# Other places in a pass for the statistics, convolution and projection products and their VectorE steps

## The chip, the core and the metric

One core of one Trainium2 chip runs the whole program. The metric is the device time of an execution in microseconds (us). Five engines work beside each other, each through its own instructions in the order of the program: TensorE (PE, matrix products), VectorE (DVE), ScalarE (ACT), GpSimd (POOL) and SyncE (SP, which here only issues transfers). They wait for one another through semaphores.

## The reference

Four residual layers stand on an input of 256 images, 256 channels and 7 x 7 positions. Each normalises its input in 32 groups of 8 channels before its own work:

```
def _gn(v, G=32, eps=1e-05):
    ...
    m = jnp.mean(g, axis=(2, 3, 4), keepdims=True)
    s = jnp.var(g, axis=(2, 3, 4), keepdims=True)
    return ((g - m) / jnp.sqrt(s + eps)).reshape(v.shape)
...
x = x + _L0_conv_ref(_gn(x), ...)   # 1x1 convolution with gathered weights
x = x + _L1_conv_ref(_gn(x), ...)   # qkv, depthwise 5x5 and grouped 1x1 of it, linear attention, projection
x = x + _L2_conv_ref(_gn(x), ...)   # a gate for each group and position
x = x + _L3_conv_ref(_gn(x), ...)   # softmax attention over positions
```

The second layer computes `qkv`, from it `agg` (depthwise 5 x 5, then a grouped 1 x 1 product), and for each of 48 heads of the two together `relu(q) (relu(k) v)`, divided by its last column; a projection follows.

## The kernel before

The images go through in 16 chunks of 16. Three phases follow one another: a setup, `layer_one_phase` (layers 0 and 1, and the statistics of layer 2) and `gate_and_attention_phase`. The change is in `layer_one_phase` alone.

That phase is one sequence of steps `g`, written out by each engine for itself. Eight steps make a pass `c = g // 8`; `u = g % 8` is the step in the pass. In passes 0 to 15 (the first half) a pass does the attention on the `qkv` of chunk `c`; in passes 16 to 31 (the second half) that on `agg`. An attention step is spread over five steps of the sequence: PE makes two `qkv` products and turns `q` (L351, L361), then the `vk` product of two steps before (L392), the output product of three steps before (L404) and the turn of the output of four steps before (L413). ACT copies the `qkv` products out of their banks (L667), the `q` (L686), the two `v` (L673) and the turned output `o` (L711); DVE makes `kT` (L492), the masked `vk` pair (L499, L503) and the normalised output (L509 to L514).

Each step has three slots, `a` (PE: after the `qkv` products, DVE: after `kT`), `b` (after the output product; after the `vk` pair) and `c` (after the output's turn; after the normalised output). Two tables, `PE_AT` and `V_AT`, say what else is done in which slot. "5c" below is slot c of step 5 in a pass. An entry is (what, number, how many passes ahead of its own chunk's). For a chunk and layer `k` (0 or 1) the chain is:

- DVE `sum` (L533), PE `stat` (a product with a mask, L437), DVE `centre` (reads the mean, L537, then subtracts it, L547), ACT `a_square` (L722), DVE `square_sum` (L552), PE `stat` again, DVE `var` (L555), ACT `a_root` (L728), DVE `scale` (four short instructions from L561 on, then L571).
- After layer 0's chain: PE `l0` (four convolution products, L445), each read by DVE (L577), whose result is the input of layer 1's chain. After layer 1's chain the next pass's `qkv` products can begin.
- For the chunk of the pass before: PE `proj` (four projection products, L452), read by DVE (L588).

The `stat`, `l0` and `proj` products, and those for the gate, share two PSUM banks in turn. Before a product writes its bank, PE waits until the product two turns before has been read:

```
            i = turn[what, n, k]
            bank = p_g[i % 2]
            wait(pe, pg_read, i - 1)
```

`turn` is counted from `PE_AT`. ACT's squares and roots have their places in `a_step`, by `u`. One buffer `sq` takes all squares, and `stat[:, 0]` and `stat[:, 1]` take both the sum and the square sum of a layer in turn.

From step 4 of pass 8 to step 2 of pass 15, and again in the second half's first 44 steps, there are fills: depthwise products of PE (L426, two or three a step), which go to one bank and are copied out by ACT (L694) before the next may start. Their input is gathered by POOL (L834) and their weights come by DMA.

Of the kernel before, what the change touches and what calls it, by code (L numbers as in the profile page):

```python
# [191 lines left out]
def layer_one_phase(nc, bass, mybir, ins, W, dram, chunks):  # L192
# [8 lines left out]
    with ctx:  # L201
        def sb(name, shape):
            return ctx.enter_context(nc.sbuf_tensor(name, shape, f32))
# [26 lines left out]
        stat = sb("stat", [128, 2, KT * NB])  # L230
        mean = sb("mean", [128, KT, NB])
        var = sb("var", [128, KT * NB])
# [73 lines left out]
        def fill_in(g, slot):  # L306

            mine = fills.get(g, [])
            return mine[slot] if slot < len(mine) else None

        PE_AT = {(0, "a"): [("stat", 1, 1)], (1, "c"): [("l0", 0, 1)], (2, "a"): [("gate_stat", 0, -2), ("l0", 1, 1)], (2, "b"): [("l0", 2, 1)],
                 (3, "a"): [("l0", 3, 1)], (5, "c"): [("gate_stat", 1, -2)],
                 (4, "b"): [("stat", 2, 1)], (4, "c"): [("proj", 0, -1)],
                 (6, "a"): [("stat", 3, 1), ("stat", 0, 2)], (6, "b"): [("proj", 1, -1)], (6, "c"): [("proj", 2, -1)],
                 (7, "b"): [("proj", 3, -1)]}
        V_AT = {(0, "a"): [("proj", 3, -2)], (0, "b"): [("var", 0, 1)], (0, "c"): [("gate_sum", 0, -2)],
# [3 lines left out]
                (5, "b"): [("proj", 0, -1), ("sum", 0, 2)], (5, "c"): [("square_sum", 1, 1)],  # L320
                (6, "b"): [("var", 1, 1), ("centre", 0, 2)], (6, "c"): [("proj", 1, -1)],
                (7, "a"): [("scale", 1, 1)], (7, "b"): [("proj", 2, -1)], (7, "c"): [("gate_scale", 0, -2), ("square_sum", 0, 2)]}

        def due(table, g, slot):

            for what, k, ahead in table.get((g % UN, slot), ()):
                n = g // UN + ahead
                if what == "proj":
                    here = 0 <= n < NP2
                elif what.startswith("gate"):  # L330
                    here = chunks <= n < NP2
                else:
                    here = 0 <= n < chunks
                if here:
                    yield what, n, k

        turn = {}
        for g in range(FIRST, LAST + 1):
            for slot in "abc":
                for key in due(PE_AT, g, slot):  # L340
                    turn[key] = len(turn)
# [88 lines left out]
        def pe_group(pe, what, n, k):  # L430
# [4 lines that stand above are left out]
            if what == "stat":  # L435
                pe.wait_ge(summed[k // 2], 2 * n + k % 2 + 1)
                mm = pe.matmul(bank[:, 0:KT * NB], W["mask8"][:, :], stat[:, k // 2, :], start=True, stop=True)  # L437
            elif what == "gate_stat":
                pe.wait_ge(gate_summed, 2 * (n - chunks) + k + 1)
                mm = pe.matmul(bank[:, 0:KT * NB], W["mask8"][:, :], stat[:, k, :], start=True, stop=True)  # L440
            elif what == "l0":
                m, h = k // 2, k % 2
                pe.wait_ge(scaled[0], n + 1)
                for t in range(KT):
                    mm = pe.matmul(bank[:, 0:HALF], W["w_sub"][:, t, 128 * m:128 * m + 128],  # L445
                                   y[:, t, HALF * h:HALF * h + HALF], start=(t == 0), stop=(t == KT - 1))
            else:
                m, h = k // 2, k % 2
                pe.wait_ge(o_ev, UN * (n + 1))
                q0 = 0 if n < chunks else 2  # L450
                for e in range(2):
                    mm = pe.matmul(bank[:, 0:HALF], W["w_proj"][:, q0 + e, 128 * m:128 * m + 128],  # L452
                                   o[:, n % 2, e, HALF * h:HALF * h + HALF], start=(e == 0), stop=(e == 1))
            mm.then_inc(pg_mm, 1)

        def pe_slot(pe, g, slot):
            for what, n, k in due(PE_AT, g, slot):
                pe_group(pe, what, n, k)
# [181 lines left out]
        def v_slot(v, g, slot):  # L640
            for what, n, k in due(V_AT, g, slot):
                if what.startswith("gate"):
                    v_gate(v, what, n)
                else:
                    v_group(v, what, n, k)
# [69 lines left out]
        def a_square(a, n, k):  # L715
            a.wait_ge(centred[k], n + 1)

            if k == 1:
                a.wait_ge(summed[0], 2 * n + 2)
            elif n > 0:  # L720
                a.wait_ge(summed[1], 2 * n)
            a.activation(sq[:, :, :], y if k == 0 else z[n % 2], ACT.Square).then_inc(squared[k], 1)  # L722
# [25 lines left out]
        def a_step(a, g):  # L748
            c, u = g // UN, g % UN

            def fill(slot):
                F = fill_in(g, slot)
                if F is not None:
                    a_fill(a, F)

            for F in fills.get(g - 1, ()):
                if F % DB_FILLS == DB_FILLS - 1:
                    a_store_agg(a, F // DB_FILLS)

            G = g - 1  # L760
            if 0 <= g < GA:
                a_raw(a, g, 0)
            if 0 <= G < GA:
                a_q(a, G)
            if 0 <= g < GA:
                a_raw(a, g, 1)
            if u == 5 and 0 <= c + 1 < chunks:
                a_square(a, c + 1, 1)
            if 0 <= G < GA:
                a.wait_ge(raw_ev, 2 * G + 2)  # L770
                a_v(a, G, raw[:, G % UN // 4, G % 4, 256:384, :].rearrange("r n q -> r q n"))
            elif GA <= G < GT:
                a_kv_of_agg(a, G)
                a_q(a, G)
            fill(0)
            fill(1)
            if 0 <= g - 4 < GT:
                a_out(a, g - 4)
            fill(2)
            if u == 2 and 0 <= c < chunks:  # L780
                a_residual(a, c)
            if u == 6 and 0 <= c + 2 < chunks:
                a_square(a, c + 2, 0)
            if u == 3 and chunks <= c - 2 < NP2:
                a_gate_square(a, c - 2 - chunks)
            if u == 6 and chunks <= c - 2 < NP2:
                a_gate_root(a, c - 2)
            if u in (0, 6) and 0 <= c + 1 < chunks:
                a_root(a, c + 1, u // 6)


# [927 lines left out]
```

## Time and profile before

| | |
|---|---|
| median of 3 runs | 2079.17 us (2075.14 to 2084.48) |
| the profiled execution | 2083.96 us, of it 2082.1 us span from the first to the last instruction |
| busy share of the span | PE 86%, DVE 66%, ACT 43%, POOL 13% |
| setup, and wait for the first chunk | to 69 us |
| first half (passes 0 to 15) | 69 to 922 us |
| second half and the end of the phase | 922 to about 1568 us |
| gate and attention phase | from about 1568 us |

The numbers of the trace are us from the span's start. "Idle before" is the time an engine did nothing before an instruction, with the one whose end released it. The granted clock is PE's, as a share of full speed (2.4 GHz; 0.50 is 1.2 GHz). A pass of the first half is measured from the first `qkv` product on its chunk to the first on the next; the product reads `half_a` and `z_odd` in turn.

### The profile page before, as it was taken

Reading aid. Unit: us, or ns where it says so; the run is one execution under the profiler, and the core shown is the slowest. Engines: PE = TensorE matmul, PEld = TensorE weight load, DVE = VectorE, ACT = ScalarE, POOL = GpSimd, SP = SyncE. Lnnn points to the kernel's source line nnn. Section 1 sums busy time; section 2 is a strip of 40 time slices with the busy share of each in tenths; the row PEclk is TensorE's granted clock in tenths of the full one; section 3 lists DMA queues with packets and bytes.
Section 4 is the critical chain, followed back from the end, with each engine's and each line's share of the span. In section 5 each row is a group of like instructions: output and inputs, shape, how many; then the busy total and the mean of one; then the engine's idle time right before and its main releaser. Section 6 shows DMA issues by size and latency. Waiting matters only on the chain. (4 is left out here: it accounts for less than half of the span.)

```text
span 2082.1 us, 42128 instructions
## 1 busy us (share of the span) xinstructions
PE 1786.3 (86%) x16164; PEld 1195.1 (57%) x16164; DVE 1372.3 (66%) x2786; ACT 901.7 (43%) x2341; POOL 277.0 (13%) x189
## 2 busy tenths in 40 slices
PE   2699999999999999997877888999983499999998
PEld 1355555555555555565555666666661366666666
DVE  4677777666555556442333447777875899999994
ACT  0344454454554544453433445455541144444343
POOL 1000000001111101002111110000001233333331
PEclk9899999999999999998988899999995699999999
DMA  3112222237666667479988986545513001111101
GB/s 100 39 63 78 101 94 78 78 125 185 207 170 199 201 160 215 145 185 218 237 231 219 246 229 166 134 121 149 156 48 128 16 32 63 62 63 63 47 32 47
DMA packets 199916, 267.17 MB, mean 128 GB/s; under 512 B 108516, under 2 KB 159588, under 8 KB 199720
## 3 DMA queue, kind: packets, MB, share of 16 engines
q1 hardware_dynamic: 189320, 225.68, 38.4%
q10 hardware_dynamic: 10240, 38.54, 6.0%
q8 instruction: 132, 2.16, 0.4%
q14 instruction: 64, 0.52, 0.1%
q0 software_dynamic: 160, 0.26, 0.0%
HBM read 148.84 MB, written 115.61 MB: 127 GB/s over the span
## 5 line engine op out<-in xcount | busy, mean ns | idle before, releaser
L499 DVE TENSOR_TENSOR vk<-p_vk,mask_vo 128x512 f32<-128x512 f32 x256 | 176.4, 689 | 478.3 <-PE p_vk L392 478.3
L426 PE MATMUL p_dw<-tw,q 98*64 98x98 f32 x3072 | 198.3, 266 | 86.8 <-ACT agg_out L694 34.9
L834 POOL COPY q<-qd 98x768 f32<-98x768 f32 x128 | 110.5, 900 | 1085.5 <-DMA qd<-qkv_scratch 787.2
L667 ACT ACTIVATE half_b<-p_qkv 98x384 f32<-98x384 f32 x256 | 134.2, 524 | 244.2 <-PE p_qkv L351 229.6
L426 PEld LDWEIGHTS p_dw<-tw,q 98*64 98x64 f32 x3072 | 148.1, 143 | 151.5 <-issue 67.8
L694 ACT ACTIVATE agg_out<-p_dw 128x294 f32<-128x294 f32 x256 | 106.9, 417 | 258.6 <-PE p_dw L426 246.0
L452 PE MATMUL p_g<-o,w_proj 128*128 128x392 f32 x512 | 207.5, 531 | 3.4 <-DVE var L555 2.8
L351 PE MATMUL p_qkv<-w_qkv,half_a 128*98 128x384 f32 x512 | 193.8, 502 | 6.7 <-DVE half_a L571 6.7
L351 PE MATMUL p_qkv<-w_qkv,z_odd 128*98 128x384 f32 x512 | 190.2, 494 | 1.8 <-DVE z_odd L571 1.8
L404 PE MATMUL p_out<-vk,qr 128*49 128x136 f32 x2048 | 170.5, 287 | 8.5 <-DVE oN L514 5.4
L711 ACT ACTIVATE o<-p_turn 128x196 f32<-128x196 f32 x256 | 85.5, 334 | 167.5 <-PE p_turn L413 166.1
L1360 PE MATMUL p_b<-wv,z 128*98 128x256 f32 x512 | 121.2, 385 | 8.0 <-DVE x L1235 8.0
L413 PE MATMUL p_turn<-ident,oN 128*128 128x128 f32 x512 | 111.1, 300 | 19.1 <-ACT qr L686 17.4
L673 ACT ACTIVATE vT<-half_b,image_of 98x256 f32<-98x256 f32 x256 | 124.4, 538 | 0.0
L404 PEld LDWEIGHTS p_out<-vk,qr 128*49 128x49 f32 x2048 | 110.3, 125 | 24.3 <-issue 10.0
L452 PEld LDWEIGHTS p_g<-o,w_proj 128*128 128x128 f32 x512 | 91.8, 199 | 56.2 <-issue 16.8
L392 PEld LDWEIGHTS p_vk<-vT,kT 98*32 98x32 f32 x4096 | 71.6, 109 | 89.4 <-issue 85.0
L392 PE MATMUL p_vk<-vT,kT 98*32 98x66 f32 x4096 | 114.2, 228 | 3.4 <-DVE vk L503 3.2
L514 DVE TENSOR_TENSOR oN<-p_out,rden 128x256 f32<-128x256 f32 x256 | 108.6, 424 | 8.8
L351 PEld LDWEIGHTS p_qkv<-w_qkv,half_a 128*98 128x98 f32 x512 | 81.0, 174 | 57.4 <-issue 47.0
L351 PEld LDWEIGHTS p_qkv<-w_qkv,z_odd 128*98 128x98 f32 x512 | 79.8, 171 | 50.7 <-issue 44.9
L673 ACT ACTIVATE vT<-p_qkv,image_of 98x256 f32<-98x256 f32 x256 | 106.9, 474 | 0.0
(192 smaller groups left out, 3202.4 us busy)
## 6 DMA issues: line engine op xcount, KB each, us to landing
qkv_scratch<-half_b SPq DMA_DIRECT2D x32, 1176.0 KB
qd<-qkv_scratch SPq DMA_DIRECT2D x64, 588.0 KB
agg_scratch<-agg_out ACTq DMA_DIRECT2D x128, 294.0 KB, 5.8
tw<-in_w_toep SPq DMA_DIRECT2D x128, 220.5 KB
half_a<-agg_scratch SPq DMA_DIRECT2D x48, 392.0 KB, 6.9
half_b<-agg_scratch SPq DMA_DIRECT2D x48, 392.0 KB, 6.8
half_a<-in_x SPq DMA_DIRECT2D x16, 784.0 KB, 4.9
x_scratch<-xb SPq DMA_DIRECT2D x16, 784.0 KB, 4.8
```

Source lines behind the costliest of these rows:

```text
L351: mm = pe.matmul(p_qkv[r][0:PR, 0:QKV], z[c % 2][:, t, PR * w:PR * w + PR], W["w_qkv"][:, t, QKV * e:QKV * e + QKV], start=(t == 0), stop= ...
L392: mm = pe.matmul(p_vk[32 * c:32 * c + 32, 2 * VC * pr:2 * VC * pr + 2 * VC], kT[:, G % 2, pr, 32 * c:32 * c + 32], vT[:, G % 2, pr, :, c, ...
L404: mm = pe.matmul(out_of[64 * i:64 * i + S, pr, 0:VO], qr[:, G % 4, at:at + S], vk[:, G % 2, pr, i, :], start=True, stop=True)
L413: mm = pe.transpose(turned_of[:, pr, 0:128], oN[:, G % 2, pr, :], W["ident"][:, :])
L426: mm = pe.matmul(p_dw[NP * cp:NP * cp + NP, PR * s:PR * s + PR], q2[:, U % Q2, DB_CH * cp + 3 * (f % DB_FILLS) + s, :, :].rearrange("r w q ...
L452: mm = pe.matmul(bank[:, 0:HALF], W["w_proj"][:, q0 + e, 128 * m:128 * m + 128], o[:, n % 2, e, HALF * h:HALF * h + HALF], start=(e == 0), ...
L499: v.tensor_tensor(dst[:, :, 0:128].rearrange("p k (c n) -> p k c n", c=HC), src[:, :, 0:2 * D].unsqueeze(2).to_broadcast([128, 4, HC, 2 * D]),
L514: v.tensor_tensor(oN[:, G % 2, :, :].rearrange("p r (h d) -> p r h d", h=8), out_of[:, :, 0:128].rearrange("p r (h d) -> p r h d", h=8), r ...
L667: a.activation(raw[:, e, g % 4, :, r], p_qkv[r][0:PR, 0:QKV], ACT.Copy).then_inc(raw_ev, 1)
L673: a.activation(vT[:, G % 2, :, i, :, 0:2 * D], src.rearrange("r q (c n) -> r q c n", c=HC), ACT.Copy, scale=W["image_of"][:, i:i + 1]).the ...
L834: g.tensor_copy(q2[:, U % Q2, DB_CH * cp:DB_CH * cp + DB_CH, :, :].rearrange("r n w q -> r w n q"), qd[:, :, at:at + DB_CH, :]).then_inc(q ...
L1360: mm = pe.matmul(p_b[0:PR, n % 2, C * q:C * q + C], two_images(z3[it % Z3S][:, t, :], 2 * n + q), wv[:, t, :], start=(t == 0), stop=(t == ...
```

## The change

Only places change. In the first half, layer 0's chain for the next chunk starts half a step to one step later: `sum` from 5b to 5c, its `stat` from 6a to 6c, `centre` from 6b to 7b, the square from the end of step 6 to the end of step 0 of the next pass, `square_sum` from 7c to 0c, its `stat` from 0a to 1a, `var` from 0b to 1b, `scale` from 1a to 1c. The four `l0` products go from 1c, 2a, 2b, 3a to 2b, 2c, 3a, 3b. In layer 1's chain `square_sum` goes from 5c to 5b, ahead of the next chunk's `sum`. In both halves the projection products 2 and 3 go from 6c and 7b to 7a and 7c on PE; DVE reads them where it did. Of the tables two lines are shown, with the lines of `a_step`:

```diff
-                (5, "b"): [("proj", 0, -1), ("sum", 0, 2)], (5, "c"): [("square_sum", 1, 1)],
...
+                (5, "b"): [("proj", 0, -1), ("square_sum", 1, 1)], (5, "c"): [("sum", 0, 2)], (6, "a"): [("gate_var", 0, -2)],
...
-            if u == 6 and 0 <= c + 2 < chunks:
-                a_square(a, c + 2, 0)
+            if u == 0 and 0 <= c + 1 < chunks:
+                a_square(a, c + 1, 0)
...
-            if u in (0, 6) and 0 <= c + 1 < chunks:
+            if u in (1, 6) and 0 <= c + 1 < chunks:
                 a_root(a, c + 1, u // 6)
```

The line numbers of the changed kernel are two lower from there on. PE, step 6 of pass 1 from its slot a and most of step 7, before (`p_g` is a bank of the shared pair; L437 `stat`, L452 `proj`):

```order
L437 MATMUL p_g<-stat,mask 128x32 x2
L392 MATMUL p_vk<-vT,kT 32x66 x8
L404 MATMUL p_out<-vk,qr 49x136 x4
L452 MATMUL p_g<-o,w_proj 128x392 x2
L413 MATMUL p_turn<-ident,oN 128x128 x2
L452 MATMUL p_g<-o,w_proj 128x392 x2
L351 MATMUL p_qkv<-w_qkv,z_odd 98x384 x2
L361 MATMUL p_turn<-ident,half_b 128x98 x2
L351 MATMUL p_qkv<-w_qkv,z_odd 98x384 x2
L392 MATMUL p_vk<-vT,kT 32x66 x8
L404 MATMUL p_out<-vk,qr 49x136 x4
L452 MATMUL p_g<-o,w_proj 128x392 x2
```

The same stretch of the changed kernel (L435 `stat`, L450 `proj`):

```order
L435 MATMUL p_g<-stat,mask 128x32
L390 MATMUL p_vk<-vT,kT 32x66 x8
L402 MATMUL p_out<-vk,qr 49x136 x4
L450 MATMUL p_g<-o,w_proj 128x392 x2
L411 MATMUL p_turn<-ident,oN 128x128 x2
L435 MATMUL p_g<-stat,mask 128x32
L349 MATMUL p_qkv<-w_qkv,z_odd 98x384 x2
L359 MATMUL p_turn<-ident,half_b 128x98 x2
L349 MATMUL p_qkv<-w_qkv,z_odd 98x384 x2
L450 MATMUL p_g<-o,w_proj 128x392 x2
L390 MATMUL p_vk<-vT,kT 32x66 x8
L402 MATMUL p_out<-vk,qr 49x136 x4
```

The next chunk's `stat` stands at the step's end instead of beside the fourth one, projection product 2 after the `qkv` products of step 7 instead of before them, and product 3 behind the turn that follows the last row.

DVE, step 5 from the `vk` pair and the first part of step 6, in the same pass, before (L533 `sum`, L552 `square_sum`, L537 and L547 `centre`):

```order
L499 TENSOR_TENSOR vk<-p_vk,mask_vo 128x4x128
L503 TENSOR_TENSOR vk<-p_vk,mask_vo 128x4x8
L588 SCALAR_TENSOR_TENSOR xb<-p_g,bn_scale,xb 128x392
L533 TENSOR_REDUCE stat<-half_a 128x32
L509 TENSOR_SCALAR den<-p_out 128x16
L511 RECIPROCAL rden<-den 128x16
L514 TENSOR_TENSOR oN<-p_out,rden 128x256
L552 TENSOR_REDUCE stat<-sq 128x32
L492 TENSOR_SCALAR kT<-half_b 98x256
L499 TENSOR_TENSOR vk<-p_vk,mask_vo 128x4x128
L503 TENSOR_TENSOR vk<-p_vk,mask_vo 128x4x8
L555 TENSOR_SCALAR var<-p_g 128x32
```

The same of the changed kernel (L531 `sum`, L550 `square_sum`):

```order
L497 TENSOR_TENSOR vk<-p_vk,mask_vo 128x4x128
L501 TENSOR_TENSOR vk<-p_vk,mask_vo 128x4x8
L586 SCALAR_TENSOR_TENSOR xb<-p_g,bn_scale,xb 128x392
L550 TENSOR_REDUCE stat<-sq 128x32
L507 TENSOR_SCALAR den<-p_out 128x16
L509 RECIPROCAL rden<-den 128x16
L512 TENSOR_TENSOR oN<-p_out,rden 128x256
L531 TENSOR_REDUCE stat<-half_a 128x32
L490 TENSOR_SCALAR kT<-half_b 98x256
L497 TENSOR_TENSOR vk<-p_vk,mask_vo 128x4x128
L501 TENSOR_TENSOR vk<-p_vk,mask_vo 128x4x8
L553 TENSOR_SCALAR var<-p_g 128x32
```

The two reductions have changed places around the normalised output.

ACT, from the end of step 6 of pass 1 to the end of step 0 of pass 2, before (L711 `o`, L722 the square, L728 the root):

```order
L711 ACTIVATE o<-p_turn 128x196
L722 ACTIVATE sq<-half_a 128x1568
L728 ACTIVATE std<-var 128x32
L667 ACTIVATE half_b<-p_qkv 98x384
L686 ACTIVATE qr<-p_turn 128x196
L667 ACTIVATE half_b<-p_qkv 98x384
L673 ACTIVATE vT<-half_b,image_of 98x2x4x32 x2
L711 ACTIVATE o<-p_turn 128x196
L667 ACTIVATE half_b<-p_qkv 98x384
L686 ACTIVATE qr<-p_turn 128x196
L667 ACTIVATE half_b<-p_qkv 98x384
L673 ACTIVATE vT<-half_b,image_of 98x2x4x32 x2
```

The changed kernel, from the root in step 6 on (L709 `o`, L720 the square, L726 the root):

```order
L726 ACTIVATE std<-var 128x32
L665 ACTIVATE half_b<-p_qkv 98x384
L684 ACTIVATE qr<-p_turn 128x196
L665 ACTIVATE half_b<-p_qkv 98x384
L671 ACTIVATE vT<-half_b,image_of 98x2x4x32 x2
L709 ACTIVATE o<-p_turn 128x196
L665 ACTIVATE half_b<-p_qkv 98x384
L684 ACTIVATE qr<-p_turn 128x196
L665 ACTIVATE half_b<-p_qkv 98x384
L671 ACTIVATE vT<-half_b,image_of 98x2x4x32 x2
L709 ACTIVATE o<-p_turn 128x196
L720 ACTIVATE sq<-half_a 128x1568
```

The square stands behind the copy of `o` in step 0 of pass 2, where the first layer's root stood before; that root is now a step later.

## Rows read from the trace of the kernel before

**Rows 1.** Windows: length, busy (count) by engine, granted clock (PEclk), DMA share, GB/s.

```profile
256.82:303.95 47.13, 44.98 (x330) 25.82 (x329) 34.31 (x77) 23.87 (x54) 0.00 (x0) 1.00 0.25 87
111.66:448.57 336.91, 321.61 (x2296) 184.01 (x2297) 241.17 (x536) 166.50 (x377) 0.00 (x0) 0.98 0.23 82
448.57:755.45 306.88, 290.29 (x2651) 178.56 (x2649) 177.78 (x382) 150.69 (x354) 42.86 (x48) 0.96 0.68 189
755.45:875.87 120.42, 114.54 (x1113) 71.16 (x1111) 68.65 (x151) 60.81 (x146) 14.53 (x16) 1.00 0.58 169
1262.00:1420.00 158.00, 143.81 (x1678) 107.77 (x1682) 121.37 (x304) 81.04 (x229) 0.00 (x0) 1.00 0.58 150
```

**Rows 2.** Time line of PE, step 6 of pass 4: start, length; idle before.

```profile
290.54 0.46 PE L361 MATMUL p_turn<-ident,half_b 98*128 98x98 f32 x2 [0.51 <-ACT o L711]
...
293.53 0.60 PE L437 MATMUL p_g<-stat,mask 128*128 128x32 f32 x4 [1.24 <-DVE stat L552]
...
295.51 1.58 PE L452 MATMUL p_g<-o,w_proj 128*128 128x392 f32 x4 [0.41 <-DVE var L555]
```

**Rows 3.** Time line of DVE, step 5 of the same pass.

```profile
289.08 1.78 DVE L533 TENSOR_REDUCE stat<-half_a 128x32 f32<-128x1568 f32 x1
...
291.61 1.78 DVE L552 TENSOR_REDUCE stat<-sq 128x32 f32<-128x1568 f32 x1
```

**Rows 4.** Time lines of PE and ACT, step 1 of pass 4; a square.

```profile
261.08 1.45 PE L351 MATMUL p_qkv<-w_qkv,half_a 128*98 128x384 f32 x4
...
263.96 0.44 PE L392 MATMUL p_vk<-vT,kT 98*32 98x66 f32 x16
...
265.20 1.52 PE L445 MATMUL p_g<-half_a,w_sub 128*128 128x392 f32 x4
...
265.40 0.34 ACT L711 ACTIVATE o<-p_turn 128x196 f32<-128x196 f32 x1
...
250.45 1.50 ACT L722 ACTIVATE sq<-half_a 128x1568 f32<-128x1568 f32 x1
```

**Rows 5.** Time lines of DVE and PE before the first attention step.

```profile
42.57 0.35 DVE L561 RECIPROCAL root<-std 128x32 f32<-128x32 f32 x1 [0.30 <-ACT std L728]
...
59.55 1.77 DVE L552 TENSOR_REDUCE stat<-sq 128x32 f32<-128x1568 f32 x1
62.11 0.19 DVE L555 TENSOR_SCALAR var<-p_g 128x32 f32<-128x32 f32 x1 [0.79 <-PE p_g L437]
...
66.25 0.35 DVE L561 RECIPROCAL root<-std 128x32 f32<-128x32 f32 x1 [1.70 <-ACT std L728]
...
69.17 4.75 PE L351 MATMUL p_qkv<-w_qkv,half_a 128*98 128x384 f32 x8 [6.66 <-DVE half_a L571]
```

**Rows 6.** Time line of PE, four waits in pass 0.

```profile
77.71 1.55 PE L445 MATMUL p_g<-half_a,w_sub 128*128 128x392 f32 x4 [0.81 <-DVE half_a L571]
...
103.20 0.60 PE L437 MATMUL p_g<-stat,mask 128*128 128x32 f32 x4 [0.70 <-DVE stat L552]
...
109.47 0.41 PE L413 MATMUL p_turn<-ident,oN 128*128 128x128 f32 x2 [0.58 <-ACT qr L686]
...
111.66 1.53 PE L351 MATMUL p_qkv<-w_qkv,z_odd 128*98 128x384 f32 x4 [1.78 <-DVE z_odd L571]
```

**Rows 7.** Time lines of ACT and PE in pass 13, with fills.

```profile
762.58 0.22 ACT L728 ACTIVATE std<-var 128x32 f32<-128x32 f32 x1
...
765.11 0.44 PE L392 MATMUL p_vk<-vT,kT 98*32 98x66 f32 x16
...
767.14 0.73 PE L426 MATMUL p_dw<-tw,q 98*64 98x98 f32 x12 [0.47 <-POOL q L834]
...
798.98 0.73 PE L426 MATMUL p_dw<-tw,q 98*64 98x98 f32 x12 [1.62 <-ACT agg_out L694]
```

**Rows 8.** Time line of PE in the second half, end of a pass.

```profile
1308.89 1.48 PE L452 MATMUL p_g<-o,w_proj 128*128 128x392 f32 x4
...
1314.12 1.04 PE L377 MATMUL p_qkv<-pwbd,half_b 128*98 128x128 f32 x8
```

More of the change, by code:

```diff
@@ L309, in fill_in @@
             return mine[slot] if slot < len(mine) else None
[L311 to L316, printed above, removed]
[3 rows of a table removed]
-                (5, "b"): [("proj", 0, -1), ("sum", 0, 2)], (5, "c"): [("square_sum", 1, 1)],
-                (6, "b"): [("var", 1, 1), ("centre", 0, 2)], (6, "c"): [("proj", 1, -1)],
-                (7, "a"): [("scale", 1, 1)], (7, "b"): [("proj", 2, -1)], (7, "c"): [("gate_scale", 0, -2), ("square_sum", 0, 2)]}
+        PE_AT = {(1, "a"): [("stat", 1, 1)], (2, "a"): [("gate_stat", 0, -2)], (2, "b"): [("l0", 0, 1)], (2, "c"): [("l0", 1, 1)],
[3 rows of a table added]
+        V_AT = {(0, "a"): [("proj", 3, -2)], (0, "c"): [("gate_sum", 0, -2), ("square_sum", 0, 1)], (1, "b"): [("var", 0, 1)],
+                (1, "c"): [("scale", 0, 1)], (2, "c"): [("gate_centre", 0, -2), ("l0", 0, 1)], (3, "a"): [("l0", 1, 1)],
+                (3, "b"): [("l0", 2, 1)], (3, "c"): [("l0", 3, 1), ("sum", 1, 1)], (4, "c"): [("gate_square_sum", 0, -2), ("centre", 1, 1)],
+                (5, "b"): [("proj", 0, -1), ("square_sum", 1, 1)], (5, "c"): [("sum", 0, 2)], (6, "a"): [("gate_var", 0, -2)],
+                (6, "b"): [("var", 1, 1)], (6, "c"): [("proj", 1, -1)], (7, "a"): [("scale", 1, 1)],
+                (7, "b"): [("centre", 0, 2), ("proj", 2, -1)], (7, "c"): [("gate_scale", 0, -2)]}
         def due(table, g, slot):
```

6 rows, old and new, of tables (PE_AT, V_AT) are left out of this document.

## The prediction

> **What bounds the kernel now.** I read the busy times and the granted clock by stretches first, then the waits of TensorE (PE), then the time lines of PE, VectorE (DVE) and ScalarE (ACT) in one pass. All the moved steps lie in layer one, and nearly all that counts in its first half (69 to 922 us), where a pass of eight steps handles one chunk of 16 images. There PE is the bound. In a pass without fills at full clock it is busy 44.98 of 47.13 us, while DVE is busy 34.31 and ACT 23.87 [rows 1]. So a microsecond counts only if PE stood idle in it, or if a wait makes it stand idle.
>
> The idle 2.15 us of such a pass all lies in step 6, in three waits [rows 2], which come back within 0.01 us in each of passes 1 to 7:
> - 0.51 us before the q transpose, for ACT. ACT has just squared the second layer's chunk in step 5, and its copy of `o` is late.
> - 1.24 us before the fourth statistics product. DVE takes the next chunk's sum (from 289.08) ahead of the square sum that PE waits for (from 291.61) [rows 3].
> - 0.41 us before projection product 1, for DVE's read of that product's bank.
>
> There is a second price. Seven passes took 336.91 us, and seven times 47.13 is 329.91. The 7.0 us between them are almost all time at half clock: the granted clock over the stretch is 0.98, not 1.00 [rows 1]. By the same view pass by pass, a stretch at half of full speed (1.2 GHz) follows the three waits in passes 1, 2, 5 and 7, and none in 3, 4 and 6: 7.0 / 4, about 1.7 us lost each time.
>
> From step 4 of pass 8 on, PE also makes the fills (depthwise products), and passes take about 60 us. There PE waits mostly for ACT's eviction of the fill before; one such wait, of about 1.6 us, comes in step 5 of nearly every pass [rows 7].
>
> **The change part by part.** No instruction is added or dropped; steps change places. The second table of order rows shows the heart of it: square sum ahead of sum.
>
> Step 6, passes without fills. The square sum takes the sum's place and can start there (289.08, not 291.61) or as soon as ACT's square ends, over 2 us earlier than now [rows 3]; the 1.24 us go. Projection product 1 now has the fourth product's bank behind it by one more product, so its 0.41 us go too. The 0.51 us stay: the second square keeps its place in step 5.
>
> Step 7. Projection product 3 now needs the bank that the next chunk's mean is read from, and DVE gets to that read only after the `vk` pair. It is the wait of 0.41 us again, with one more pair of transposes on PE ahead of it: 0.2 us, an estimate.
>
> Steps 0 and 1. The first layer's square moves from the end of ACT's step 6 to the end of its step 0, its square sum from DVE's 7c to 0c, and its product from PE's 0a to 1a. This chain used to be spread over a step and a half of slack; now it follows itself closely. A step with nothing extra takes PE 4.12 us (261.08 to 265.20), and ACT starts its copy of `o` 4.32 us into it [rows 4]. So the square starts at 4.32 + 0.34 = 4.66 after step 0 begins, ends 1.50 later, and from the start of a square sum to the product that needs it 1.92 us pass (291.61 to 293.53) [rows 2 to 4]: the product can start at 8.08. PE is there at 4.12 + 2.88 = 7.00 (2.88 is 261.08 to 263.96). A new wait of 1.1 us. DVE is behind the same square, so the scaling after it, moved to 1c, ends level with PE's arrival at the first convolution product in 2b: 0.1 us, an estimate. Queued behind DVE's wait at 0c are the `kT` of step 1 and the scaling, for which PE waits no longer than said. Behind the square on ACT stands the eviction of step 1's first qkv product, and PE needs that bank only in step 2. No DMA moves; SP's loads and stores wait for the same steps as before.
>
> Per pass without fills: 0.5 + 0.2 + 1.1 + 0.1 = 1.9 in place of 2.15. Seven passes: -1.8 us. The wait is moved rather than removed.
>
> Passes with fills (8 to 14). In step 6 there is nothing to win, for PE shows no wait at its statistics product there. The new wait is there all the same: ACT is free at 762.58 (where it now takes the first root), so the product could start at 762.58 + 1.50 + 1.92 = 766.00, and PE is there at 765.11 [rows 7]: 0.9 us. The product's own 0.2 us come on top, since in step 0 a fill waits for ACT anyway and taking the product out wins nothing. ACT catches up during the wait, so most of the 0.47 us at the next fill goes [rows 7]: minus 0.3. Moving the convolution and projection products changes which fills have a product between them; I make that level. 0.8 us, seven times: +5.6 us. Bounds: nothing (if fills hide it) and 1.2.
>
> The start. Before the first attention step PE waits for a chain on DVE and ACT alone. Now the next chunk's centring and its square stand between the variance (62.11) and its root, and the reciprocal starts at 66.25 [rows 5]. After the change the square sum starts at 59.55 as before, the sum follows (1.70 each, as between the starts in rows 3 and what comes behind), the variance is read at 62.95, and the reciprocal follows 0.19 + 0.30 later, as in the first round [rows 5]: 63.44. -2.8 us. Pass 0 then loses its waits of 0.81, 0.70, 0.58 and 1.78 [rows 6] and gets 1.1 (the new one), 0.35 (first convolution product) and about 1.0 in step 6, where no projection product yet separates the two statistics products and DVE has still the sum, `kT`, `vk` and the variance to do: -1.4 us.
>
> The second half (922 to 1568 us). Only projection products 2 and 3 move on PE. Now product 2 starts at 1308.89, as the last of step 6, and the next pass at 1314.12 [rows 8]. Taking product 2 behind the pointwise products of step 7 and product 3 to that step's end leaves the same work between these two times, and DVE's `vk`, which follows PE's, starts when it did. 0; with fills 0.2 us a pass either way.
>
> The clock. The half-clock stretches in passes 1 to 7 came after three waits close together, 2.15 us within 6. Afterwards the longest cluster is 1.1 us. In neither half did I find one behind a wait of 1.2 us or less that stands apart: from 1262 us on PE is idle 14.2 of 158 us, in waits of about 1 us and less, and the clock is 1.00 [rows 1]. So I take the four stretches as gone: -7.0 us. In passes 8 to 12 the mean clock is 0.96 over 306.88 us, which costs some 0.04 of it, 12 us, in stretches behind waits of 1.6 to 2.0 us; after 755 us the same waits, as the 1.62 us at 798.98, cost no clock (1.00) [rows 1, 7]. I leave those as they are.
>
> **Sum.** -1.8 + 5.6 - 2.8 - 1.4 - 7.0 = -7.4 us. The profiled execution took 2083.96 us (span 2082.1): 2076.6, say 2077. The median of the runs shown is 2079.17, 4.8 below this execution, which may come of fewer half-clock stretches, so less is left to win against it. I call the change level with the median; 0.5% is 10.4 us, about what a measurement of this kernel tells from no change.
>
> **Rivals.**
> 1. The clock stays as it was in passes 1 to 7. The 0.51 us stay and the new wait is nearly as long as the old. For it: identical waits gave a stretch in four passes and not in three. 2083.96 - 0.4 = 2083.6.
> 2. The new wait is hidden, and with it the cluster. If ACT reaches the square sooner than I place it, and the looser order keeps the fill passes at full clock as well: 2076.6 - 5.6 - 12 = 2059; half of both, 2068. Against it: the 1.6 us wait in step 5 has a cause that isn't touched.
> 3. Slower: the short waits throttle every pass. A wait of 1.1 us at the product of step 1, in the middle of a pass that has the 0.51 or the 1.6 us as well, could bring a stretch of half clock to each. At 1.7 us a stretch, seven instead of four in passes 1 to 7 and six more in the fill passes: 2083.6 + 5.1 + 10.2 = 2099. It decides from four added stretches on (2090). Against it: waits in pass 0 of up to 1.78 us were not followed by one [rows 6]. The Trainium skill, page "TensorE: Matmul & The Clock Gate", section "A second HAM failure mode: psum-queue depth-cycling", says that short, frequent idle spells of PE between groups of matmuls can make the clock swing between its two levels, which would give this rival's time; the trace agrees only for waits of 1.5 us and more or for several close together.
> 4. The reorder doesn't reach PE. If the fourth product still comes late because ACT's square ends late, 1.24 us of each pass come back: 2076.6 + 8.7 = 2085. DVE now finds the square done when it comes to it, without a wait [rows 3], so little speaks for it.
>
> **How the numbers follow.** My forecast has 0.45 (its own range 2070 to 2084), rival 1 0.18, rival 2 0.21, rival 3 0.13, rival 4 0.03. Three quarters of rival 2 and a tenth of the forecast lie under 2068.8 (0.20 together); rival 3 lies over 2089.6 (0.13); the rest is within 0.5%. The range of 8 in 10 takes in most of rivals 2 and 3: 2062 to 2091.
>
> **What would show it.** Right: no wait for the square sum in step 6; a wait of about 1 us at the first-layer statistics product of step 1 in nearly every pass up to 14; the first qkv product some 2.8 us earlier; passes 1 to 7 near 46.9 us each, at clock 1.00; fill passes 0.8 us longer at equal clock; the second half the same length. Wrong: fill passes no longer or even shorter, half-clock stretches behind step 1, or a new wait of PE on DVE at the convolution products of step 2.

## The result and the profile after

The changed kernel took 2064.86 us (median of 7 runs, 2060.7 to 2070.3) against 2079.17 us for the kernel before on the same chip (7 runs, 2071.57 to 2084.48): a ratio of 0.9943 [0.992, 0.9965], 0.57% faster (in brackets the 95% interval; the plain quotient of the two medians is 0.9931). The forecast was 2077 us, level with the median; the time lies in its range (2062 to 2091), and just over the bound of 0.5% on the fast side. The profiled execution took 2067.97 us, with a span of 2066.2 in place of 2082.1.

Stretch by stretch, each of the first half measured between the same two `qkv` products in both traces:

| stretch | before | after | difference | forecast |
|---|---|---|---|---|
| start, to the first `qkv` product | 69.17 | 67.65 | -1.5 | -2.8 |
| pass 0 | 42.49 | 40.62 | -1.9 | -1.4 |
| passes 1 to 7 | 336.91 | 326.62 | -10.3 | -8.8 (-1.8 and -7.0) |
| passes 8 to 14 | 427.30 | 429.45 | +2.2 | +5.6 |
| pass 15 | 46.01 | 46.37 | +0.4 | none made |
| second half and last phase | 1160.2 | 1155.5 | -4.7 | 0 |
| sum | | | -15.9 | -7.4 |

The last row runs from the first pointwise product to the end. The windows of the changed kernel that answer to [rows 1] (same columns): pass 0, passes 1 to 7, pass 4 alone, passes 8 to 12, passes 13 and 14.

```profile
67.65:108.27 40.62, 38.47 (x246) 21.00 (x246) 27.03 (x54) 21.40 (x47) 0.00 (x0) 0.94 0.15 50
108.27:434.89 326.62, 316.03 (x2297) 180.67 (x2298) 243.25 (x534) 167.07 (x379) 0.00 (x0) 1.00 0.25 87
248.42:295.04 46.62, 45.12 (x329) 25.79 (x328) 34.60 (x77) 23.82 (x54) 0.00 (x0) 1.00 0.25 87
434.89:740.70 305.81, 286.02 (x2650) 175.81 (x2648) 180.91 (x383) 150.73 (x354) 45.38 (x48) 0.98 0.67 191
740.70:864.34 123.64, 116.41 (x1111) 72.03 (x1110) 70.83 (x153) 61.61 (x145) 14.75 (x16) 0.99 0.53 158
```

Read the granted clock, the third number from the right, first. It is 1.00 over the whole of passes 1 to 7, where it was 0.98. A pass there is 46.62 us instead of 47.13, and PE is idle 1.50 of it instead of 2.15.

The time line of PE in pass 4 and at the start of pass 5 (start, length; idle before), which answers to [rows 2]: the turn of `q` in step 6, the two statistics products of that step (the one for the square sum, then the one for the next chunk's sum), projection product 3 at the end of step 7, and the first layer's product for its square sum, now in step 1.

```profile
283.35 0.45 PE L359 MATMUL p_turn<-ident,half_b 98*128 98x98 f32 x2 [0.50 <-ACT o L709]
...
284.93 0.30 PE L435 MATMUL p_g<-stat,mask 128*128 128x32 f32 x2
...
287.78 0.31 PE L435 MATMUL p_g<-stat,mask 128*128 128x32 f32 x2
...
293.62 1.58 PE L450 MATMUL p_g<-o,w_proj 128*128 128x392 f32 x4
...
303.06 0.38 PE L435 MATMUL p_g<-stat,mask 128*128 128x32 f32 x2 [0.95 <-DVE stat L550]
```

The 0.50 stays, the 1.24 and the 0.41 of [rows 2] are gone, and a wait of 0.95 has come, 20 us further on. What releases it is told by ACT and DVE in the same step 0 of pass 5 (time lines of the two engines):

```profile
299.36 0.33 ACT L709 ACTIVATE o<-p_turn 128x196 f32<-128x196 f32 x1
299.59 1.50 ACT L720 ACTIVATE sq<-half_a 128x1568 f32<-128x1568 f32 x1
...
301.13 1.79 DVE L550 TENSOR_REDUCE stat<-sq 128x32 f32<-128x1568 f32 x1 [1.09 <-ACT sq L720]
```

DVE waits 1.09 us for the square, and PE waits for DVE: the chain runs from ACT to DVE to PE without slack, as the prediction placed it. Step 0 began at 295.04, so `o` is at 4.32, the square at 4.55 (4.66 was forecast) and the product at 8.02 (8.08 was forecast).

The time line of PE in pass 9, with fills:

```profile
494.36 0.73 PE L424 MATMUL p_dw<-tw,q 98*64 98x98 f32 x12 [0.80 <-ACT agg_out L692]
...
499.19 0.38 PE L435 MATMUL p_g<-stat,mask 128*128 128x32 f32 x2 [0.95 <-DVE stat L550]
...
532.61 0.84 PE L424 MATMUL p_dw<-tw,q 98*64 98x98 f32 x12 [1.64 <-ACT agg_out L692]
```

And windows of 2 us behind its last wait (columns as in [rows 1]):

```profile
533.00:535.00 2.00, 2.00 (x23) 1.40 (x18) 1.93 (x5) 0.75 (x2) 0.00 (x0) 0.52 0.73 277
535.00:537.00 2.00, 2.00 (x7) 0.98 (x4) 1.33 (x2) 0.42 (x1) 1.67 (x2) 0.50 0.43 112
```

The new wait came in each fill pass (0.95 us, in two of them 0.87; 6.5 us over the seven), and the clock stayed full behind it. The clock fell to 0.50 (1.2 GHz) behind the wait of 1.64 us for ACT's eviction, which the change does not touch. This happened in passes 9, 12 and 13. Taking one minus the clock times the length, pass by pass, about 8.4 us went to half clock in passes 8 to 14, against 11.8 before: -3.4 by the clock and +5.5 by the rest, where +5.6 was forecast. The parts of that rest agree less well than its sum: PE's waits for ACT's eviction fell from 19.3 to 15.2 us, and its waits for POOL rose from 0.9 to 2.9, of which one in pass 12 is 2.01.

The start, time line of DVE: the reads of the four groups of convolution products, then the sum, the variance and the reciprocal that [rows 5] showed before.

```profile
48.69 0.63 DVE L575 SCALAR_TENSOR_TENSOR half_a<-p_g,b_sub,half_a 128x392 f32<-128x392 f32 x1 [3.13 <-PE p_g L443]
51.30 0.63 DVE L575 SCALAR_TENSOR_TENSOR half_a<-p_g,b_sub,half_a 128x392 f32<-128x392 f32 x1 [1.99 <-PE p_g L443]
52.95 0.62 DVE L575 SCALAR_TENSOR_TENSOR half_a<-p_g,b_sub,half_a 128x392 f32<-128x392 f32 x1 [1.03 <-PE p_g L443]
54.27 0.63 DVE L575 SCALAR_TENSOR_TENSOR half_a<-p_g,b_sub,half_a 128x392 f32<-128x392 f32 x1 [0.69 <-PE p_g L443]
...
62.58 1.78 DVE L531 TENSOR_REDUCE stat<-half_a 128x32 f32<-128x1568 f32 x1
64.27 0.18 DVE L553 TENSOR_SCALAR var<-p_g 128x32 f32<-128x32 f32 x1
64.75 0.35 DVE L559 RECIPROCAL root<-std 128x32 f32<-128x32 f32 x1 [0.29 <-ACT std L726]
```

The sixteen convolution products of PE that these reads follow, in the changed kernel and in the one before, and the last of the four reads before:

```profile
45.70 8.53 PE L443 MATMUL p_g<-half_a,w_sub 128*128 128x392 f32 x16 [3.52 <-DVE half_a L569]
...
45.58 7.30 PE L445 MATMUL p_g<-half_a,w_sub 128*128 128x392 f32 x16 [3.53 <-DVE half_a L571]
...
52.91 0.63 DVE L577 SCALAR_TENSOR_TENSOR half_a<-p_g,b_sub,half_a 128x392 f32<-128x392 f32 x1 [0.69 <-PE p_g L445]
```

From the last of the four reads to the first `qkv` product (67.65) it is now 13.38 us; before, it was 16.26. That is -2.88, the forecast's -2.8. But the four reads themselves span 5.58 us here and spanned 4.34 before, since the sixteen products took 8.53 us in place of 7.30, and so 1.24 came back.

The last row of the table is left open. Windows of before, from the first pointwise product to the end in two parts:

```profile
921.88:1575.00 653.12, 552.57 (x6517) 410.41 (x6515) 367.30 (x916) 285.78 (x803) 53.09 (x64) 0.93 0.68 179
1575.00:2082.00 507.00, 410.46 (x2900) 293.63 (x2900) 439.17 (x644) 184.66 (x549) 157.15 (x48) 0.92 0.15 55
```

The same of the changed kernel:

```profile
910.71:1560.00 649.29, 547.89 (x6516) 407.25 (x6514) 366.70 (x916) 285.99 (x803) 53.74 (x64) 0.94 0.69 179
1560.00:2066.00 506.00, 409.02 (x2900) 292.78 (x2900) 439.97 (x645) 184.68 (x549) 157.16 (x48) 0.93 0.16 56
```

The same products cost PE 6.1 us less (956.9 against 963.0) at a clock 0.01 higher, and the other engines as much as before. Together with the seven profiles below there are nine, one of each kernel. In the four with projection products 2 and 3 at their old places this stretch takes 1160.2 to 1163.3 us, in the five with the new places 1154.9 to 1159.7. By one minus the clock times the length, 86 to 90 us of it went to half clock in the four, and 78 to 85 in the five. So the -4.7 may come of the change, by way of the clock, and not of a difference between executions alone. With one profile of each kernel, and only about 0.5 us between the two groups, that is not shown.

### The profile page after: what moved, and what is told of

Its sections match the earlier page's. It is cut to its first block and busy times, and to the rows that moved or that the text cites. A ratio compares the mean times of both kernels' runs of the same rounds, so it can differ in the third digit from the quotient of the medians.

```text
span 2066.2 us, 42128 instructions
## 1 busy us (share of the span) xinstructions
PE 1773.7 (86%) x16164; PEld 1186.7 (57%) x16164; DVE 1378.0 (67%) x2786; ACT 902.2 (44%) x2341; POOL 280.4 (14%) x189
## 5 line engine op out<-in xcount | busy, mean ns | idle before, releaser
L450 PE MATMUL p_g<-o,w_proj 128*128 128x392 f32 x512 | 199.4, 514 | 0.8 <-ACT o L709 0.5
L709 ACT ACTIVATE o<-p_turn 128x196 f32<-128x196 f32 x256 | 85.5, 334 | 155.2 <-PE p_turn L411 154.4
L402 PEld LDWEIGHTS p_out<-vk,qr 128*49 128x49 f32 x2048 | 109.6, 124 | 24.3 <-issue 10.3
L450 PEld LDWEIGHTS p_g<-o,w_proj 128*128 128x128 f32 x512 | 91.8, 195 | 51.5 <-issue 11.5
```

Source lines behind the costliest of these rows:

```text
L402: mm = pe.matmul(out_of[64 * i:64 * i + S, pr, 0:VO], qr[:, G % 4, at:at + S], vk[:, G % 2, pr, i, :], start=True, stop=True)
```

## The experiments

The theory, called A in the expectations, is the prediction's mechanism as the trace after bears it out: each wait of PE counts at its length times the number of passes, an edit taken back brings its own waits back and no others, and half clock follows waits that are long or lie close together. The rival, B, lets the gain come from elsewhere; each expectation says what it would give there. The median of the kernel before beside them was 2076.99 us for the first two, the fourth and the fifth below, and 2079.4 us for the other three.

**The sum ahead of the square sum again.** In the changed kernel, the two reductions of step 5 change back:

```diff
-                (5, "b"): [("proj", 0, -1), ("square_sum", 1, 1)], (5, "c"): [("sum", 0, 2)], ...
+                (5, "b"): [("proj", 0, -1), ("sum", 0, 2)], (5, "c"): [("square_sum", 1, 1)], ...
```

> The changed kernel with one part undone: in DVE's step 5 the next chunk's sum stands ahead of the square sum again (5b and 5c as before the change); all other places stay as changed. Theory A (the swap is what PE's step 6 needed): the wait of 1.24 us at the fourth statistics product comes back in passes 1 to 7, which go from 46.6 to about 47.9 us at full clock; fill passes unchanged; the start 0.8 us shorter, since the sum no longer stands between square sum and variance: about 8 us more than the changed kernel (2073), and more (up to 12 us) if half-clock stretches come back behind the waits of 0.5 and 1.24 us. Rival B (moving the other products apart did it): no wait of 1 us in step 6, time within 2 us of the changed kernel.

Measured: 2074.93 us, ratio 0.9994 [0.9973, 1.0014]. Its window of passes 1 to 7, and its waits of PE there (us in total, times, longest):

```profile
106.60:443.24 336.64, 317.51 (x2299) 180.05 (x2297) 243.42 (x534) 166.86 (x380) 0.00 (x0) 1.00 0.24 85
```

```profile
PE p_g L435 <- DVE stat L550: 15.4, 14, 1.2
PE p_turn L359 <- ACT o L709: 3.5, 7, 0.5
```

The 1.24 us are back beside the 0.95, and the seven passes cost 10.0 us more than in the changed kernel, 8.7 of them in this wait. So the gain needs the exchange of the two reductions. And a point for the clock: PE is idle 2.7 us a pass here, more than the 2.15 before the change, and no pass has a stretch at half clock.

**That exchange alone, in the kernel before.**

```diff
-                (5, "b"): [("proj", 0, -1), ("sum", 0, 2)], (5, "c"): [("square_sum", 1, 1)],
+                (5, "b"): [("proj", 0, -1), ("square_sum", 1, 1)], (5, "c"): [("sum", 0, 2)],
```

> The kernel before with the swap alone: square sum in DVE's 5b, the next chunk's sum in 5c; all else as before the change, so that the next chunk's first statistics product still stands beside the fourth one at the head of PE's step 6. Theory A (the swap alone moves the wait to the neighbouring product, which needs the sum): PE waits 1.2 to 1.5 us at the second of the two products, passes 1 to 7 stay at 47.1 to 47.5 us plus half-clock stretches, no gain: 2077 to 2083. Rival B (the swap is the whole gain): passes 1 to 7 at 45.9 us, about 2068 or less.

Measured: 2081.11 us, ratio 1.0021 [1.0003, 1.0038]. Its waits of PE in passes 1 to 7:

```profile
PE p_g L437 <- DVE stat L533: 9.8, 7, 1.4
PE p_turn L361 <- ACT o L711: 3.5, 7, 0.5
PE p_g L452 <- DVE var L555: 2.8, 7, 0.4
...
```

The wait has only changed its name: the next chunk's statistics product, which still stands in 6a, now waits 1.4 us for the sum (L533). Three of seven passes had a stretch of half clock (335.84 us in all), and the first `qkv` product came at 71.60, 2.4 later; half of that stands in its sixteen convolution products, which took 8.50 us. So the exchange by itself gains nothing as long as that product stays in 6a. No run has the exchange with that product in 6c and nothing else changed.

**Projection products 2 and 3 back.** In the changed kernel, on PE alone:

```diff
-                 (6, "c"): [("stat", 0, 2)], (7, "a"): [("proj", 2, -1)], (7, "c"): [("proj", 3, -1)]}
+                 (6, "c"): [("stat", 0, 2), ("proj", 2, -1)], (7, "b"): [("proj", 3, -1)]}
```

> The changed kernel with projection products 2 and 3 back at their old places on PE (6c, behind the next chunk's first statistics product, and 7b); all else as changed. Theory A (these moves matter in the first half only, where product 2 would wait for DVE's read of product 1, and product 3 for the read of the mean): new waits of about 0.8 us in step 6 and 0.5 us in step 7, passes 1 to 7 at about 47.9 us in place of 46.6, fill passes up to 0.8 us longer; the stretch from 922 us on (there 1155 to 1160 us in all runs so far) unchanged: 8 to 14 us more than the changed kernel, ratio to the kernel before 0.998 to 1.002. Rival B (their move brought the 4 us that the changed kernel's second half and last phase are shorter in the first profile): the second half 4 us longer, passes 1 to 7 unchanged, ratio 0.996.

Measured: 2077.43 us, ratio 1.0 [0.9973, 1.0027]. Its waits of PE in passes 1 to 7:

```profile
PE p_g L435 <- DVE stat L550: 6.7, 7, 1.0
PE p_g L450 <- DVE xb L586: 5.7, 7, 0.8
PE p_turn L359 <- ACT o L709: 3.5, 7, 0.5
PE p_g L450 <- DVE mean L535: 2.8, 7, 0.4
...
```

Two waits for the shared pair of banks appear, 0.8 and 0.4 us: the product has arrived before DVE has read the one two turns before. The second half, where the same two products went back, took 1160.3 us to the end. That is 4.8 us more than in the changed kernel, about what B expected there, while passes 1 to 7 did not stay unchanged, as B had it; one profile does not settle the second half (see above). So the places of the projection products, which look like a side matter of the change, cost as much as the exchange wins: 1.24 us a pass, 8.7 in passes 1 to 7, and 1.8 in the fill passes (431.21).

**The new wait taken away: the first layer's square a step earlier.** In the changed kernel ACT squares at the end of step 7 of the pass before, instead of at the end of step 0:

```diff
-            if u == 0 and 0 <= c + 1 < chunks:
-                a_square(a, c + 1, 0)
+            if u == 7 and 0 <= c + 2 < chunks:
+                a_square(a, c + 2, 0)
```

> The changed kernel with the first layer's square one place earlier on ACT: at the end of step 7, right behind the centring it needs, in place of the end of step 0. Theory A (the wait of 0.95 us at the statistics product of step 1 is the chain copy of o, square, square sum): the square sum no longer waits, the product of step 1 finds it done, passes 1 to 7 take about 45.7 us, passes 8 to 14 0.7 to 0.9 us less each: 14 us less than the changed kernel, about 2051. Rival B (the square's 1.5 us on ACT only make something else late, as the second layer's square does with 0.5 us and 1.6 us): a new wait of 0.5 to 1.5 us for ACT in step 0, time 2058 to 2065.

Measured: 2051.95 us, ratio 0.9884 [0.9861, 0.9908]. Windows of passes 1 to 7 and of passes 8 to 14:

```profile
107.50:426.46 318.96, 314.39 (x2296) 180.72 (x2297) 242.40 (x534) 168.32 (x379) 0.00 (x0) 1.00 0.25 89
426.46:854.97 428.51, 405.42 (x3759) 250.84 (x3757) 250.42 (x536) 214.06 (x499) 60.18 (x64) 0.97 0.63 182
```

The 0.95 us are gone from every pass (45.42 us each but the first), and nothing takes their place but 0.65 us in pass 1. In the fill passes the wait is gone too, but the profiled execution lost more there to half clock (six of the seven passes have a stretch) and was, at 2062.5, the slowest of this kernel's six. The ratio moved by 0.0059 against the changed kernel's, 12 us, and 0.95 us in 14 passes are 13.3.

**The other wait: the second layer's square first in step 5.** In the changed kernel ACT squares before it copies the `qkv` products of step 5:

```diff
+            if u == 5 and 0 <= c + 1 < chunks:
+                a_square(a, c + 1, 1)
             if 0 <= g < GA:
                 a_raw(a, g, 0)
...
                 a_raw(a, g, 1)
-            if u == 5 and 0 <= c + 1 < chunks:
-                a_square(a, c + 1, 1)
```

> The changed kernel with the second layer's square moved to the start of ACT's step 5, ahead of the evictions of the qkv products, instead of between them and the two v copies. Theory A (the 0.5 us wait at the q transpose of step 6 and the 1.6 us wait at a fill of step 5 both come from this square's place on ACT, and the half-clock stretches of the fill passes from that 1.6 us wait): 0.5 us less in passes 1 to 8, 1.2 us less in passes 8 to 14, and those passes at clock 1.00 (8 us more in this profile): 12 us from the waits and up to 8 from the clock, about 2045 to 2053. Rival B (the qkv evictions get late in its place, or DVE's centring is not done by then): 2060 to 2070. On the clock alone: if half-clock stretches in the fill passes remain without waits of 1.6 us, that wait was not their cause.

Measured: 2051.12 us, ratio 0.9882 [0.9855, 0.991]. Windows as for the last kernel, and the waits of PE in passes 8 to 14:

```profile
107.41:430.63 323.22, 315.93 (x2298) 181.29 (x2297) 242.08 (x534) 166.93 (x380) 0.00 (x0) 1.00 0.25 88
430.63:844.22 413.59, 394.71 (x3759) 244.10 (x3757) 249.54 (x536) 212.54 (x499) 61.10 (x64) 1.00 0.66 188
```

```profile
PE p_g L435 <- DVE stat L550: 6.5, 7, 1.0
PE p_dw L424 <- ACT agg_out L692: 6.0, 13, 1.1
PE p_dw L424 <- POOL q L832: 3.6, 4, 2.2
```

The 0.50 us are gone (46.17 a pass). More is won in the fill passes, -15.9 us: the waits for ACT's eviction were 15.2 us in 14 with a longest of 1.7, and are 6.0 with a longest of 1.1. The granted clock is 1.00 in each of the seven passes. So that wait of 1.6 us in step 5 was the square's doing: the eviction stood behind it on ACT. One wait of 2.2 us, for POOL, was not followed by half clock.

**The same edit in the kernel before.** It tells whether the last gain needs the change.

> The kernel before with only the second layer's square moved to the start of ACT's step 5; the sum stays ahead of the square sum. Theory A (in passes 1 to 7 DVE's sum sets when the fourth statistics product can start, so a wait that ends before it is covered by it): the 0.5 us wait at the q transpose goes, the wait at the statistics product grows from 1.24 to about 1.75 us, the passes stay at 47.1 us at full clock, half-clock stretches stay as likely; the fill passes lose their 1.6 us wait, 1.2 us each, and run at clock 1.00: 9 us from the waits and up to 8 from the clock, ratio to the kernel before 0.991 to 0.996. Rival B (the 0.5 us is a price of its own): passes 1 to 7 at 46.6 us and no half-clock stretch in them, ratio 0.985 or less.

Measured: 2077.14 us, ratio 0.9982 [0.9959, 1.0004]. Passes 1 to 7, the waits of PE there, and two windows of 2 us in pass 4:

```profile
111.35:454.16 342.81, 327.37 (x2297) 188.61 (x2298) 241.69 (x537) 165.94 (x377) 0.00 (x0) 0.96 0.23 81
```

```profile
PE p_g L437 <- DVE stat L552: 14.2, 8, 2.0
...
PE p_g L452 <- DVE var L555: 1.2, 3, 0.4
```

```profile
296.00:298.00 2.00, 2.00 (x10) 1.13 (x7) 1.97 (x5) 0.00 (x0) 0.00 (x0) 0.50 0.03 8
298.00:300.00 2.00, 2.00 (x6) 1.11 (x5) 1.60 (x5) 0.00 (x0) 0.00 (x0) 0.50 0.00 0
```

The 0.51 us are gone, and the statistics product waits 1.99 us instead of 1.24: PE only comes earlier to a square sum that DVE still takes second. The fill passes win as before (411.74 us, clock 1.00 in six of seven; the seventh has a wait of 2.79 us for nothing that the profile shows), but now all seven passes without fills have a stretch of half clock, and cost 5.9 us more. That the clock would get worse there was not expected, and the time missed its range for that.

**Both squares moved, in the changed kernel** (the two edits above together).

> The changed kernel with both squares moved on ACT as in the two runs before (first layer's at the end of step 7, second layer's at the start of step 5). Theory A (the two waits are independent): passes 1 to 7 at 45.0 us, passes 8 to 14 at about 59 us and clock 1.00, the gains add: 13 + 13 us less than the changed kernel, about 2038 on the first chip, ratio to the kernel before 0.981 to 0.984. Rival B (with one wait gone the other engine's work shows: ACT or DVE is late somewhere else in the fill passes): ratio 0.985 to 0.988.

Measured: 2034.62 us, ratio 0.9791 [0.9761, 0.9822], faster than both kernels. Windows of passes 1 to 7 and of passes 8 to 14:

```profile
105.68:421.32 315.64, 314.39 (x2299) 181.31 (x2298) 241.53 (x534) 168.20 (x380) 0.00 (x0) 1.00 0.26 90
421.32:827.96 406.64, 392.97 (x3760) 244.58 (x3758) 248.87 (x536) 213.74 (x499) 60.08 (x64) 1.00 0.66 192
```

PE is idle 1.25 us in seven passes, and a pass is 45.00 us. In the profiles the two gains add: passes 1 to 7 take 11.0 us less than in the changed kernel, against 7.7 and 3.4 for the two edits by themselves. The ratio came out below the expected 0.981 to 0.984. The fill passes take 22.8 us less, and all have kept full clock, where the kernel with the first square alone had half clock in six of seven; that this made the difference to the expectation is likely, not shown. This is the fastest version measured here.

## Why the prediction was right, and where it was off

**The wait is moved rather than removed: right.** The 1.24 us went with the exchange (the first experiment brought them back), the 0.41 with the spacing of the projection products, the 0.50 stayed, and the chain of square, square sum and product made a wait of 0.95 us (1.12 in pass 0, 0.87 in two fill passes) where 1.1 was forecast, in all passes up to 14. The two small estimates were wrong: the 0.2 us for projection product 3 and the 0.1 us at the first convolution product did not appear in these passes. The idle time of a pass came to 1.50 and not 1.9, while PE's busy time rose by 0.14 (45.12 against 44.98). At full clock the seven passes won 3.3 us, where -1.8 stood in the sum.

**The clock in passes 1 to 7: right.** The four stretches are gone, -7.0 us as forecast. The reason given fits the later runs: groups of three waits within 6 us brought stretches in the kernel before (four) and with the exchange alone (three), and the 0.50 and 1.24 us in the first experiment, without the third wait, brought none. Nor was it a matter of the two profiled executions: over whole runs the recorded clock has a median of 0.954 in the changed kernel (seven runs), and of 0.949 and 0.948 in two sets of 23 runs of the kernel before. Of 2070 us, 0.005 is about 10 us, an estimate, and an upper one, as it counts idle time at half clock too.

**Pass 0: -1.9 for -1.4, by other parts.** The four waits went, and 1.12 and 0.32 us came, as forecast; the 1.0 us in step 6 did not come. Against that, about 0.4 us more went to half clock at its start.

**Fill passes: the term was right at equal clock, +5.5 for +5.6, in part by luck.** The new wait was there (6.5 us, 6.3 forecast), but ACT's eviction gave back 4.1 us where 2.1 stood in the sum, and 2.0 us more of waiting for POOL, which the prediction did not have, made up for that. The clock there was left as it was; it gave 3.4 us back in the profiled execution. Half clock followed three of the seven waits of 1.6 to 1.7 us for ACT's eviction, and it vanished in both changed kernels that shortened these waits. So here it comes of them. How many of them are followed by one differs from profile to profile: it was three passes of seven here and six in the kernel with the first square moved, which has the same waits for ACT's eviction in step 5. The prediction called their cause untouched by the change, which the trace bears out.

**The start: right in kind, half in size.** The chain on DVE and ACT is 2.88 us shorter; 1.24 were lost to slower convolution products, which nothing in the change explains. These sixteen products took 7.39 to 8.39 us in the other four kernels with the same start, and 7.13 to 8.50 in the kernel before and the two made from it, so they differ from profile to profile by as much as this.

**The second half: open.** The forecast was 0; it took 4.7 us less in the profile. The nine profiles fall into two groups by the places of projection products 2 and 3, and the time at half clock goes with them, so a gain of some 4 us there, which the prediction put at nothing, is possible and not shown.

**The step that failed is the last one of the sum**, from -7.4 us to "level with the median", for it took the lower median as a sign that less was left to win against it. The medians fell by 14.3 us, nearly as much as the profiled executions by 16.0. Taken off the median, the sum would have given 2071.8 and not 2077. The rest, 6.9 us by the medians and 8.6 by the profiles, lies in the terms themselves. Set too small were passes 1 to 7 (by 1.5 us), the clock of the fill passes (3.4) and, if it is the change's doing, the second half (4.7); the start was set too large (1.3). The four half-clock stretches of the profiled execution of before seem no exception of that execution: the kernel with the exchange alone had three, that with the second square moved had seven, and the clock over whole runs, given above, differs by as much.

**The rivals.** The first (the clock stays) and the fourth (the reorder doesn't reach PE) fell by the windows and by the missing wait. The second gave the time more nearly than the forecast did (half of it was 2068), but not by its mechanism: the new wait is not hidden, and the fill passes did not keep full clock. The third, that short waits throttle every pass, fell: no stretch of half clock stands behind the new wait of 0.87 to 0.95 us, in 14 passes. The Trainium skill's rule that was set beside it (page "TensorE: Matmul & The Clock Gate", section "A second HAM failure mode: psum-queue depth-cycling") says that short, frequent idle spells can make the clock swing; the traces agree in part. Half clock followed many of the waits of 1.5 us and more, and some of the groups of three within 6 us; in passes 1 to 14 it followed no wait of 1.24 us or less that stood alone or in a pair.

## What to carry to other kernels

An exchange of two steps on one engine is worth what the step that now comes second can afford: here the gain needed the exchange, the later place of the product that reads the second result, and projection products spread so that no bank is asked for too early. The exchange alone gave nothing, and neither did the change without the exchange or without that spread. Follow each wait of the bounding engine back to the queue that held it up: both waits left after the change came from a square of 1.50 us on ACT, which is idle for nearly half of each pass (busy 23.82 of 46.62), and moving the two by a step or less was worth more than the change itself (0.9943 to 0.9791). Read the granted clock by stretches before costing a wait: here the same group of waits cost 2.15 us in three passes, and about 1.6 us more, at half clock, in four.

## What the runs showed of the hardware that was not expected

The idle time of a pass in itself did not decide on the clock; its lengths and places went with it. Over passes 1 to 7, one profile of each kernel, by waits of PE in a pass (us; a bar stands between waits over 9 us apart):

| kernel | waits in a pass | passes with half clock |
|---|---|---|
| before | 0.51, 1.24, 0.41 | 4 of 7 |
| exchange alone | 0.50, 1.40, 0.41 | 3 of 7 |
| before, second square first | 1.99, in three passes 0.41 behind it | 7 of 7 |
| changed | 0.50 \| 0.95 | 0 of 7 |
| sum first again | 0.50, 1.24 \| 0.95 | 0 of 7 |
| projection products back | 0.51, 0.82, 0.41 \| 0.95 | 0 of 7 |

The kernel with the most idle time (the sum first again, 2.7 us a pass) kept full clock in all seven. The same waits at the same places were followed by half clock in some passes and not in others, and what decides in a single pass stays open. Nor does the length of a single wait decide: of the waits for POOL in the fill passes, one of 2.84 us (first square moved) came with half clock, and one of 2.68 us (both moved) did not. In the first two kernels of the table a stretch cost 1.4 to 1.7 us; in two passes of the kernel before with the second square first it lasted twice as long, and they took 49.85 us where the shortest took 48.24.

The other surprise is at the start: the sixteen convolution products took between 7.13 and 8.53 us in the nine profiles, while the granted clock reads 1.00 over the whole of the 8.53 us and the 7.30 us. DVE's reads show that the first products are the slow ones: in the changed kernel the second read starts 2.61 us after the first, and the last 1.32 us after the third. That is a pace of one half, which the record of the clock doesn't show, and the cause stays open.
